# A graph layer's start-up: the last edge targets are converted in group 24, the first transfers change queues, and two filler matmuls go

## The chip, the cores and the metric

The kernel runs on one core of a Trainium2 chip. A core has a matrix engine (TensorE, PE in the profile; its weight loads are PEld), a vector engine (VectorE, DVE), a scalar engine (ScalarE, ACT), GpSimd (POOL) and a sync engine (SyncE, SP) that here only issues transfers. Each runs its own instructions in order, and they wait for one another on semaphores. DMAs are issued by SP, ACT and POOL and carried out by 16 DMA engines. The metric is the time of one execution on the device in microseconds (us); lower is better.

## The reference

Messages run along 25,000 edges between 50,000 nodes with 128 features, all float32. `dst` is sorted. What is computed, cut to its core:

```python
msg = jax.nn.relu(x[src] + edge_attr)                     # 25,000 x 128
agg = jax.ops.segment_sum(msg, dst, num_segments=50000)
h = x + agg
h = jax.nn.relu(jax.nn.relu(h @ W1 + b1) @ W2 + b2)       # 128 -> 256 -> 128
out = layernorm(x + h)                                    # eps 1e-5, no scale
```

## The kernel before

The nodes are cut into 131 groups: 130 of 384 nodes (three tiles of 128) and a last one of 80. The edges of a group lie in one stretch of the sorted list, and the kernel takes two windows of 128 edges for a group (one for the last group). Where the windows start depends on `dst`, so the kernel first has to search.

**The start-up.** `prepare` loads the first target of each of 125 rows of 200 edges (`dst_first`, line 396), the first target of each next row (`dst_next`, 232) and all the rows (`dst_rows`, 230). VectorE compares the first targets with the groups' first nodes (361 to 367) and marks the row in which each group begins (`row_holds`). TensorE picks these rows with two matmuls (421); ScalarE has converted the rows to floats for it (401). VectorE counts in them (289) and gets the window starts (382). GpSimd then fetches each window's (source, target) pairs (119). For groups 0 and 1 the windows are known beforehand: `first_pairs` holds the first 512 pairs, and GpSimd gathers their source rows at once (127). While it waits, TensorE runs fillers whose result nobody reads (`keep_busy`, 411): six matmuls of 128 columns on the identity before the search, three and one of 256 columns behind it.

**The main path**, for each group g. GpSimd gathers the source rows (113), SP loads `edge_attr` (107) and x (102). VectorE adds source rows and edge attributes (593), ScalarE takes the rectified sum rounded (`msg_hi`, 747), VectorE the rest (`msg_lo`, 600); in groups 0, 2 and 3 the second window isn't split but used whole (`msg_whole`, 607). TensorE transposes x into PSUM (838) and adds the messages by a product with 0/1 selection matrices (865; 861 for a whole part; 887 and 891 in group 1). ScalarE copies the sum to SBUF (`copy_hT`, 753), TensorE multiplies by W1 (the first layer, 901), ScalarE adds the bias and rectifies (759), TensorE multiplies by W2 (909), and VectorE adds the bias, x and takes the statistics (616, 628, 635, 644). ScalarE takes the root (764) and normalizes (778); SP stores (517). While group g's layers run, TensorE also transposes and sums group g + 1.

The order of work on each engine is written out by hand: as straight lines for the first groups, as a loop from group 2 or 3 on. On ScalarE the first groups read as follows, with the step that the change moves in the middle (lines 784 to 797):

```python
        high_part(1, 0)
        hidden(0, 0)
        source_nodes()
        hidden(0, 1)
        high_part(1, 1)
        act.wait_ge(c["last_pairs_loaded"], 16)
        nc.scalar.activation(c["last_dst"][:, :], c["last_pairs"][:, 1:2], ACT.Copy).then_inc(last_dst_ready, 1)
        copy_hT(1)
        hidden(1, 0)
```

`last_pairs` holds the pairs of the last 128 edges. SP loads it between the transfers of groups 3 and 4 (524). Its targets, converted to float (`last_dst`, 792), are needed on VectorE when it builds the last group's selection (573), and its sources by GpSimd for the last gather.

Of the kernel before, what the change touches and what calls it, by code (L numbers as in the profile page):

```python
# [8 lines left out]
ACT = mybir.ActivationFunctionType  # L9
# [12 lines left out]
EW = 128  # L22
# [9 lines left out]

ROWS = 125
TARGETS_FOUND, TARGETS_CHECKED, CHECKED = (12, 16), 20, 30
FAR = float(1 << 20)


# [5 lines left out]
FIRST_CHUNKS = 4  # L43
# [120 lines left out]
def prepare(nc, x, edge_attr, dst, pairs, w1, b1, w2, b2, c, sb, sem):  # L164

    edges, = dst.shape
    ROW = edges // ROWS
# [17 lines left out]
    dst_first = sb("dst_first", [ROWS, 1], INT32)  # L185
# [41 lines left out]
    flags_summed = sem("flags_summed")  # L227

    def prepare_sync(sp):
        sp.dma_start(dst_rows[:, :], dst.rearrange("(r e) -> r e", e=ROW)).then_inc(dst_loaded, 16)  # L230
        sp.wait_ge(next_cleared, 1)
        sp.dma_start(dst_next[0:ROWS - 1, :], bass.AP(dst.tensor, ROW, [[ROW, ROWS - 1], [1, 1]]),
                     allow_slow_non_contiguous=True).then_inc(next_loaded, 16)
        sp.dma_start(first_pairs[:, 1:FIRST_CHUNKS, :], pairs[EW:FIRST_CHUNKS * EW, :].rearrange("(k p) a -> p k a", p=EW),
                     allow_slow_non_contiguous=True).then_inc(more_pairs_loaded, 16)
        start_x(sp, x, 0, 0, c)
        start_edge_attr(sp, edge_attr, 0, 0, c)
        sp.dma_start(c["w1_sb"][:, :], w1).then_inc(w1_loaded, 16)
        for h in range(HC):
            sp.dma_start(c["b1_sb"][:, h:h + 1], b1[h * 128:(h + 1) * 128].rearrange("(p a) -> p a", a=1)).then_inc(w1_loaded, 16)  # L240

        sp.wait_ge(c["first_loaded"][0], 16)
        start_edge_attr(sp, edge_attr, 1, K * EW, c)
        start_x(sp, x, 1, 1, c)
        sp.dma_start(c["w2_sb"][:, :, :], w2.rearrange("(c p) n -> p c n", p=128)).then_inc(w2_loaded, 16)

        sp.wait_ge(c["window_loaded"], 16)
        sp.dma_start(b2_sb[:, 0, :], b2.rearrange("(a n) -> a n", a=1).to_broadcast([128, b2.shape[0]])).then_inc(c["b2_loaded"], 16)
# [144 lines left out]
    def prepare_scalar(act):  # L393

        act.dma_start(first_pairs[:, 0, :], pairs[0:EW, :]).then_inc(pairs_loaded, 16)
        act.dma_start(dst_first[:, :], bass.AP(dst.tensor, 0, [[ROW, ROWS], [1, 1]]),
                      allow_slow_non_contiguous=True).then_inc(first_loaded, 16)
        act.wait_ge(eps_ready, 1)
        nc.scalar.activation(table_mark[:, :], eps_col[:, :], ACT.Sqrt)
        act.wait_ge(dst_loaded, 16)  # L400
        nc.scalar.activation(dst_rows_f[:, 1:ROW + 1], dst_rows[:, :], ACT.Copy).then_inc(dst_f_ready, 1)
        act.wait_ge(pairs_loaded, 16)
        act.wait_ge(more_pairs_loaded, 16)
        nc.scalar.activation(first_dst[:, :], first_pairs[:, :, 1], ACT.Copy).then_inc(first_dst_ready, 1)

    def prepare_tensor(pe):
# [6 lines left out]
                                 start=True, stop=True)  # L413

        pe.wait_ge(ident_ready, 1)
        keep_busy(6, 128)
        pe.wait_ge(dst_f_ready, 1)
        pe.wait_ge(row_of_ready, 1)
        for k in range(K):
# [15 lines left out]
def main_path(nc, x, pairs, edge_attr, out, c, sb, sem, checks):  # L435
# [301 lines left out]
    def main_scalar(act):  # L737
# [50 lines left out]
        source_nodes()  # L788
        hidden(0, 1)
        high_part(1, 1)  # L790
        act.wait_ge(c["last_pairs_loaded"], 16)
        nc.scalar.activation(c["last_dst"][:, :], c["last_pairs"][:, 1:2], ACT.Copy).then_inc(last_dst_ready, 1)
        copy_hT(1)
        hidden(1, 0)
        high_part(2, 0)
# [8 lines left out]
        for g in range(3, LAST):  # L804
# [6 lines left out]
            for t in range(T):  # L811
                if inside(g - 3):
                    last = normalize(g - 3, t)
                if t == 0 and g == END:
                    deviation(LAST - 2)
                if t == 1 and inside(g + 2):
                    high_part(g + 2)
# [508 lines left out]
```

## Time and profile before

| | |
|---|---|
| three timed runs | 476.31, 475.66, 477.24 us (median 476.31) |
| the profiled execution | 476.41 us, its span 474.6 us |
| busy share of the span | PE 97%, PEld 80%, DVE 90%, ACT 91%, POOL 67% |
| chain that ended last | PE 94%, DVE 2%, issue 1%, ACT 1%, other 1% |
| granted TensorE clock, mean of the span | 0.989 |
| HBM traffic | 60.51 MB read, 25.60 MB written |

All rows come from the one profiled execution. A start is counted from the start of the span. A busy share close to 100% means that an engine works, not that it works at its peak. The chain is followed back from the last instruction, at each step to what released it; "issue" in it is time in which an engine waited for nothing that the profile shows. Matmuls of float32 operands appear as two records each.

### The profile page before, as it was taken

What the parts mean: (1) busy time and instruction counts of PE and PEld (TensorE: products, weight loads), DVE (VectorE), ACT (ScalarE), POOL (GpSimd) and SP (SyncE); (2) the same over time, 40 slices, a digit from 0 to 9 for tenths busy, and PEclk for the clock granted to TensorE, in tenths of its full rate; (3) what the DMA queues carried; (4) which work ended last, traced back from release to release, by engine and by line L of the source; (5) the groups of instructions that cost most, each with busy time, mean ns of one, the idle gap of its engine ahead of it and who ended that gap; (6) DMA issues with size and microseconds to landing.
All of it is one profiled execution on the core that took longest, in us unless ns stands there. A gap on an engine that the chain in (4) does not pass through costs nothing.

```text
span 474.6 us, 10056 instructions
## 1 busy us (share of the span) xinstructions
PE 458.8 (97%) x3037; PEld 380.3 (80%) x3037; DVE 426.8 (90%) x1761; ACT 431.0 (91%) x1047; POOL 317.0 (67%) x280
## 2 busy tenths in 40 slices
PE   7799999999999999998999999999999999999994
PEld 6678888888788888886888888888888888888883
DVE  6679999999999999996999999999999999999996
ACT  2359999999999999996999999999999999999995
POOL 6656766677677777655577777777777777777722
PEclk9899999999999999998999999999999999999998
DMA  5636666666666666665566666666666666666632
GB/s 125 190 89 189 201 182 202 194 197 190 197 183 197 189 199 187 195 194 155 170 191 186 199 203 186 197 191 200 185 200 189 199 189 191 195 194 196 190 118 88
DMA packets 83609, 86.77 MB, mean 183 GB/s; under 512 B 11767, under 2 KB 79252, under 8 KB 83556
## 3 DMA queue, kind: packets, MB, share of 16 engines
q1 hardware_dynamic: 74786, 68.76, 47.0%
q0 software_dynamic: 8496, 17.38, 13.4%
q8 instruction: 23, 0.38, 0.3%
q14 instruction: 30, 0.25, 0.2%
q10 hardware_dynamic: 274, 0.00, 0.0%
HBM read 60.51 MB, written 25.60 MB: 181 GB/s over the span
## 4 chain that ended last, share of the span: by engine, by line
PE 94%; DVE 2%; issue 1%; ACT 1%; another core or an unknown queue 1%; POOL 0%; POOLq 0%; DVEq 0%
PE h_ps L909 37%; PE h1T_ps L901 35%; PE hT_ps L865 12%; PE hT_ps L838 9%; PE h1T_ps L411 1%; PE spare_ps L861 0%; PE prep_ps L421 0%; DVE stats L635 0%; DVE h L616 0%; DVE z L628 0%; ACT hT L753 0%; ACT std L764 0%; DVE mean_var L644 0%; DVE msg_lo L600 0%
## 5 line engine op out<-in xcount | busy, mean ns | idle before, releaser
L113 POOL DMA_INDIRECT x_src<-in_x_dram,src_of x256 | 305.7, 1194 | 135.7 <-ACT hT L753 90.7
L909 PE MATMUL h_ps<-w_sb,h1T 128*128 128x128 f32 x1564 | 200.0, 278 | 0.4 <-ACT h1T L759 0.4
L901 PE MATMUL h1T_ps<-hT,w_sb 128*128 128x384 f32 (+1 forms) x524 | 190.4, 486 | 4.3 <-issue 2.9
L909 PEld LDWEIGHTS h_ps<-w_sb,h1T 128*128 128x128 f32 x1564 | 187.8, 194 | 0.7 <-ACT h1T L759 0.6
L778 ACT ACTIVATE y<-z,shift,rstd 128x128 f32<-128x128 f32 x384 | 172.3, 481 | 0.5 <-DVE shift L655 0.5
L759 ACT ACTIVATE h1T<-h1T_ps,b_sb 128x384 f32<-128x384 f32 (+1 forms) x262 | 151.1, 578 | 19.1 <-remote 2.3
L901 PEld LDWEIGHTS h1T_ps<-hT,w_sb 128*128 128x128 f32 x524 | 89.6, 191 | 39.4 <-issue 3.8
L616 DVE TENSOR_TENSOR h<-h_ps,b_sb 128x384 f32<-128x384 f32 x131 | 72.7, 555 | 35.1 <-PE h_ps L909 29.1
L635 DVE BATCH_NORM_STATS2 stats<-z 128x6 f32<-128x128 f32 x391 | 88.7, 282 | 0.1
L838 PEld LDWEIGHTS hT_ps<-ident,x_sb 128*128 128x128 f32 (+1 forms) x379 | 49.3, 140 | 39.6 <-issue 22.8
L576 DVE TENSOR_TENSOR sel<-node_in_range,dst_of 128x432 fp32r<-128x432 f32 x127 | 76.3, 601 | 0.0
L865 PE MATMUL hT_ps<-sel,msg_hi 128*128 128x216 f32 x250 | 71.4, 311 | 2.3 <-DVE msg_lo L600 2.3
L628 DVE SCALAR_TENSOR_TENSOR z<-h,x_sb 128x384 f32<-128x384 f32 x131 | 72.2, 551 | 0.0
L753 ACT ACTIVATE hT<-hT_ps 128x384 f32<-128x384 f32 x128 | 62.5, 488 | 2.3 <-issue 1.4
L865 PE MATMUL hT_ps<-sel,msg_lo 128*128 128x216 f32 x250 | 62.6, 276 | 0.0
L838 PE MATMUL hT_ps<-ident,x_sb 128*128 128x128 f32 (+1 forms) x379 | 62.1, 272 | 0.0
L747 ACT ACTIVATE msg_hi<-pre_msg 128x256 fp32r<-128x256 f32 (+1 forms) x132 | 54.3, 411 | 5.9 <-DVE pre_msg L593 5.7
L600 DVE SCALAR_TENSOR_TENSOR msg_lo<-pre_msg,msg_hi 128x256 fp32r<-128x256 f32 (+1 forms) x132 | 54.0, 409 | 4.7 <-ACT msg_hi L747 2.6
L593 DVE TENSOR_TENSOR pre_msg<-pre_msg,x_src 128x256 f32<-128x256 f32 (+1 forms) x135 | 51.8, 384 | 0.0
L865 PEld LDWEIGHTS hT_ps<-sel,msg_hi 128*128 128x128 f32 x250 | 47.8, 191 | 2.8 <-DVE msg_lo L600 2.8
L865 PEld LDWEIGHTS hT_ps<-sel,msg_lo 128*128 128x128 f32 x250 | 48.1, 193 | 0.0
L644 DVE BATCH_NORM_AGGREGATE mean_var<-stats 128x2 f32<-128x6 f32 x391 | 40.0, 157 | 0.2
(132 smaller groups left out, 142.3 us busy)
## 6 DMA issues: line engine op xcount, KB each, us to landing
x_sb<-in_x_dram SPq DMA_DIRECT2D x130, 192.0 KB
out_dram<-y SPq DMA_DIRECT2D x130, 192.0 KB
pre_msg<-in_edge_attr_dram SPq DMA_DIRECT2D x130, 128.0 KB
x_src<-in_x_dram,src_of POOLq DMA_INDIRECT x256
w_sb<-in_w_dram SPq DMA_DIRECT2D x2, 128.0 KB
dst_rows<-in_dst_dram SPq DMA_DIRECT2D x1, 97.7 KB
x_src<-in_x_dram,first_pairs POOLq DMA_INDIRECT x4, 2.8
b_sb<-in_b_dram SPq DMA_DIRECT2D x1, 64.0 KB
```

The costliest lines, as they stand in the source:

```text
L113: nc.gpsimd.indirect_dma_start(out=c["x_src"][:, g % EB, k, :], out_offset=None, in_=x, in_offset=bass.IndirectOffsetOnAxis(ap=index, axis ...
L576: nc.vector.tensor_tensor(sel[:, g % EB, :, :], node_in_range[:, :, :].to_broadcast([128, K, T * WP]), dst_of[:, g - FIRST_ROW:g - FIRST_R ...
L616: nc.vector.tensor_tensor(h2[0:p, g % 2, 0:n, :], h2_ps[g % 2][0:p, 0:n, :], b2_sb[0:p, :, :].to_broadcast([p, n, D]), ALU.add).then_inc(h ...
L628: nc.vector.scalar_tensor_tensor(z[0:p, g % ZB, 0:n, :], h2[0:p, g % 2, 0:n, :], 0.0, x_sb[0:p, g % XB, 0:n, :], ALU.max, ALU.add).then_in ...
L635: last = nc.vector.bn_stats(stats[0:p, g % SB, t, :], z[0:p, g % ZB, t, :])
L753: nc.scalar.activation(hT[:, 0:n, 0:p], sum_bank(g)[:, 0:n, 0:p], ACT.Copy).then_inc(hT_copied, 1)
L759: nc.scalar.activation(h1T[:, h, 0:n, 0:p], h1T_ps[h][:, 0:n, 0:p], ACT.Relu, bias=b1_sb[:, h:h + 1]).then_inc(h1_ready, 1)
L778: return nc.scalar.activation(y[0:p, g % YB, t, :], z[0:p, g % ZB, t, :], ACT.Identity, bias=shift[0:p, g % SB, t:t + 1], scale=rstd[0:p, ...
L838: nc.tensor.matmul(sum_bank(g)[:, t, 0:p], x_sb[0:p, g % XB, t, :], ident[0:p, 0:p], is_transpose=True, start=(t == 0), stop=False, skip_g ...
L865: last = nc.tensor.matmul(sum_bank(g)[:, 0:n, p0:p1], part[:, g % EB, k, :], cols, start=False, stop=final, skip_group_check=True)
L901: nc.tensor.matmul(h1T_ps[h][:, 0:n, 0:p], w1_sb[:, h * 128:(h + 1) * 128], hT[:, 0:n, 0:p], start=True, stop=True).then_inc(h1_summed, 1)
L909: last = nc.tensor.matmul(h2_ps[g % 2][0:p, t, :], h1T[:, h, t, 0:p], w2_sb[:, h, :], start=(h == 0 and t == 0), stop=(h == HC - 1), skip_ ...
```

## The change

Three edits, all in the order of work; no arithmetic is changed.

- The wait for `last_pairs` and the conversion to `last_dst` leave ScalarE's straight lines between `high_part(1, 1)` and `copy_hT(1)`. They now stand in ScalarE's loop, in the round of group 24, behind the first of group 21's three normalizations.
- `dst_first` goes from ScalarE's queue to the head of SP's, ahead of `dst_rows`. `dst_next` (with its wait for the cleared column) and the second load of `first_pairs` go from SP's queue to ScalarE's, behind the first load of `first_pairs` and ahead of ScalarE's first instruction.
- The fillers ahead of the search are four matmuls instead of six.

```diff
     def prepare_sync(sp):
+        sp.dma_start(dst_first[:, :], bass.AP(dst.tensor, 0, [[ROW, ROWS], [1, 1]]),
+                     allow_slow_non_contiguous=True).then_inc(first_loaded, 16)
         sp.dma_start(dst_rows[:, :], dst.rearrange("(r e) -> r e", e=ROW)).then_inc(dst_loaded, 16)
-        sp.wait_ge(next_cleared, 1)
-        sp.dma_start(dst_next[0:ROWS - 1, :], bass.AP(dst.tensor, ROW, [[ROW, ROWS - 1], [1, 1]]),
-                     allow_slow_non_contiguous=True).then_inc(next_loaded, 16)
-        sp.dma_start(first_pairs[:, 1:FIRST_CHUNKS, :], pairs[EW:FIRST_CHUNKS * EW, :].rearrange("(k p) a -> p k a", p=EW),
-                     allow_slow_non_contiguous=True).then_inc(more_pairs_loaded, 16)
         start_x(sp, x, 0, 0, c)
...
         act.dma_start(first_pairs[:, 0, :], pairs[0:EW, :]).then_inc(pairs_loaded, 16)
-        act.dma_start(dst_first[:, :], bass.AP(dst.tensor, 0, [[ROW, ROWS], [1, 1]]),
-                      allow_slow_non_contiguous=True).then_inc(first_loaded, 16)
+        act.wait_ge(next_cleared, 1)
+        act.dma_start(dst_next[0:ROWS - 1, :], bass.AP(dst.tensor, ROW, [[ROW, ROWS - 1], [1, 1]]),
+                      allow_slow_non_contiguous=True).then_inc(next_loaded, 16)
+        act.dma_start(first_pairs[:, 1:FIRST_CHUNKS, :], pairs[EW:FIRST_CHUNKS * EW, :].rearrange("(k p) a -> p k a", p=EW),
+                      allow_slow_non_contiguous=True).then_inc(more_pairs_loaded, 16)
...
         pe.wait_ge(ident_ready, 1)
-        keep_busy(6, 128)
+        keep_busy(4, 128)
...
-        act.wait_ge(c["last_pairs_loaded"], 16)
-        nc.scalar.activation(c["last_dst"][:, :], c["last_pairs"][:, 1:2], ACT.Copy).then_inc(last_dst_ready, 1)
         copy_hT(1)
...
             for t in range(T):
                 if inside(g - 3):
                     last = normalize(g - 3, t)
+                if t == 0 and g == LAST_DST_AT:
+                    act.wait_ge(c["last_pairs_loaded"], 16)
+                    nc.scalar.activation(c["last_dst"][:, :], c["last_pairs"][:, 1:2], ACT.Copy).then_inc(last_dst_ready, 1)
```

How the instructions stand on the engines. First ScalarE's program in the first groups, before: from group 1's second rounding to group 1's second hidden half (`hT<-prep_ps1` is the copy of group 1's sum).

```order
L747 ACTIVATE msg_hi<-pre_msg 128x128 [waits sum_ready]
L792 ACTIVATE last_dst<-last_pairs 128x1 [waits last_pairs_loaded]
L753 ACTIVATE hT<-prep_ps1 128x384 [waits hT_summed]
L759 ACTIVATE h1T<-h1T_ps0,b1_sb 128x384 [waits h1_summed]
L747 ACTIVATE msg_hi<-pre_msg 128x128 [waits sum_ready]
L759 ACTIVATE h1T<-h1T_ps1,b1_sb 128x384 [waits h1_summed]
```

The same place now:

```order
L748 ACTIVATE msg_hi<-pre_msg 128x128 [waits sum_ready]
L754 ACTIVATE hT<-prep_ps1 128x384 [waits hT_summed]
L760 ACTIVATE h1T<-h1T_ps0,b1_sb 128x384 [waits h1_summed]
L748 ACTIVATE msg_hi<-pre_msg 128x128 [waits sum_ready]
L760 ACTIVATE h1T<-h1T_ps1,b1_sb 128x384 [waits h1_summed]
```

The copy of group 1's sum now follows the rounding directly. Its new place on ScalarE, in the round of group 24, where `y` is the normalized output of group 21:

```order
L760 ACTIVATE h1T<-h1T_ps1,b1_sb 128x384 [waits h1_summed]
L765 ACTIVATE std<-mean_var,eps_col 128x3 [waits var_ready]
L754 ACTIVATE hT<-hT_ps 128x384 [waits hT_summed]
L779 ACTIVATE y<-z,shift,rstd 128x128 [waits shift_ready]
L815 ACTIVATE last_dst<-last_pairs 128x1 [waits last_pairs_loaded]
L779 ACTIVATE y<-z,shift,rstd 128x128
L748 ACTIVATE msg_hi<-pre_msg 128x256 [waits sum_ready]
```

One activation was put between the first and the second tile; nothing else moved there. Last the head of SP's program, before:

```order
L230 DMA dst_rows<-in_dst_dram 125x200
L232 DMA dst_next<-in_dst_dram 124x1 [waits next_cleared]
L234 DMA first_pairs<-in_pairs_dram 128x3x2
L102 DMA x_sb<-in_x_dram 128x384
L107 DMA pre_msg<-in_edge_attr_dram 128x2x128
```

and now, where the two transfers that left stand on ScalarE's queue behind `first_pairs<-in_pairs_dram 128x2`:

```order
L231 DMA dst_first<-in_dst_dram 125x1
L233 DMA dst_rows<-in_dst_dram 125x200
L103 DMA x_sb<-in_x_dram 128x384
L108 DMA pre_msg<-in_edge_attr_dram 128x2x128
L236 DMA w1_sb<-in_w1_dram 128x256
```

The rows have moved from the first place to the second, behind a load of 125 single elements; the loads of x and what follows have one transfer fewer ahead of them.

## Rows read from the trace of the kernel before

**Rows 1.** Stretch: us; busy PE, PEld, DVE, ACT, POOL; clock; DMA share; GB/s.

```profile
100.00:200.00 100.00, 100.00 (x679) 83.04 (x678) 93.27 (x383) 96.77 (x236) 71.43 (x59) 1.00 0.64 192
```

**Rows 2.** The chain that ended last: start, us, what.

```profile
16.43 2.90 issue
19.33 1.60 PE h1T_ps L901 x4
...
23.24 2.04 PE spare_ps L861 x2
...
25.85 1.56 PE h1T_ps L901 x4
...
28.62 0.43 PE prep_ps L861 x2
...
29.72 1.47 PE h1T_ps L901 x4
...
217.75 3.10 another core or an unknown queue
```

**Rows 3.** Timeline of TensorE, last addend of group 1's sum: start, us, what.

```profile
15.42 0.34 PE L891 MATMUL prep_ps<-second_sel,msg_lo 128*128 128x384 f32 x1
```

**Rows 4.** Timeline of ScalarE: the conversion, the copy of group 1's sum.

```profile
18.69 0.20 ACT L792 ACTIVATE last_dst<-last_pairs 128x1 f32<-128x1 int32 x1 [4.16 <-DMA last_pairs<-in_pairs_dram]
18.80 0.47 ACT L753 ACTIVATE hT<-prep_ps 128x384 f32<-128x384 f32 x1
```

**Rows 5.** Busy time by stretch, 22 to 24 us; columns as in rows 1.

```profile
22.00:24.00 2.00, 2.00 (x10) 1.95 (x9) 0.24 (x2) 0.00 (x0) 1.34 (x2) 0.50 0.54 152
```

**Rows 6.** Timeline of VectorE, group 2's messages and group 0's statistics.

```profile
18.21 0.28 DVE L593 TENSOR_TENSOR pre_msg<-pre_msg,x_src 128x128 f32<-128x128 f32 x1
18.41 0.67 DVE L635 BATCH_NORM_STATS2 stats<-z 128x6 f32<-128x128 f32 x3
21.09 0.29 DVE L600 SCALAR_TENSOR_TENSOR msg_lo<-pre_msg,msg_hi 128x128 fp32r<-128x128 f32 x1 [2.01 <-issue]
21.30 0.28 DVE L593 TENSOR_TENSOR pre_msg<-pre_msg,x_src 128x128 f32<-128x128 f32 x1
21.61 0.23 DVE L607 TENSOR_SCALAR msg_whole<-pre_msg 128x128 f32<-128x128 f32 x1
```

**Rows 7.** Timeline of GpSimd, the first gather of group 3.

```profile
16.38 0.94 POOL L113 DMA_INDIRECT x_src<-in_x_dram,src_of  x1 [0.30 <-issue]
```

**Rows 8.** Of the gathered rows' tile, 0 to 40 us: time to landing.

```profile
DMA to landing us min/median/max: 2.8/2.8/2.8
```

**Rows 9.** Timeline of all engines in the start-up; SPq and ACTq are issues.

```profile
0.75 0.40 SPq L230 DMA_DIRECT2D dst_rows<-in_dst_dram  x1
...
1.17 0.64 ACTq L396 DMA_DIRECT2D dst_first<-in_dst_dram  x1
...
2.16 2.93 PE L411 MATMUL h1T_ps<-ident 128*128 128x128 f32 x12 [2.16 <-POOL ident L260]
...
3.67 0.37 ACT L401 ACTIVATE dst_rows_f<-dst_rows 125x200 f32<-125x200 int32 x1 [0.34 <-DMA dst_rows<-in_dst_dram]
4.07 0.16 DVE L361 TENSOR_TENSOR first_of<-dst_first,lowest 125x1 f32<-125x1 int32 x1 [1.83 <-DMA dst_first<-in_dst_dram]
...
4.99 0.61 DVE L367 SCALAR_TENSOR_TENSOR row_holds<-node_row,next_of,row_before 125x128 f32<-125x128 f32 x2
...
5.49 1.68 PE L421 MATMUL prep_ps<-dst_rows_f,row_holds 125*128 125x201 f32 x4 [0.40 <-issue]
```

**Rows 10.** Timeline of TensorE, a full round's second layer, and first layers.

```profile
32.09 1.51 PE L909 MATMUL h_ps<-w_sb,h1T 128*128 128x128 f32 x12
...
214.31 1.46 PE L901 MATMUL h1T_ps<-hT,w_sb 128*128 128x384 f32 x4
...
217.71 1.46 PE L901 MATMUL h1T_ps<-hT,w_sb 128*128 128x384 f32 x4
...
225.16 1.64 PE L901 MATMUL h1T_ps<-hT,w_sb 128*128 128x384 f32 x4
```

More of the change, by code:

```diff
@@ L34 @@
 TARGETS_FOUND, TARGETS_CHECKED, CHECKED = (12, 16), 20, 30
+LAST_DST_AT = 24
 FAR = float(1 << 20)
```

## The prediction

> **What bounds the kernel now.** I read the long middle stretch first, then the chain of waits, then each engine's rows in the first 30 us. In the steady part TensorE is busy without a break at the full granted clock: 100.00 us of 100 [rows 1]. There a group costs what its matmuls cost, and nothing in this change touches them. So the change can act only where TensorE stands still: in the start-up and, perhaps, at one odd stop near 218 us. The chain shows both [rows 2]: 2.90 us of "issue" before the first layer of group 1 at 19.33, and 3.10 us at 217.75. After the start-up TensorE always has its next work, so what the start-up gains stays to the end.
>
> **The wait that goes.** The last addend of group 1's sum is issued at 15.42 and takes 0.34, so the sum is complete at 15.76 [rows 3]. Its copy out of PSUM starts on ScalarE only at 18.80, because ScalarE, in order, first stands 4.16 us for the last edge targets and converts them at 18.69 [rows 4]. TensorE has run out at 16.43 and starts group 1's first layer at 19.33 [rows 2], right behind the copy. With the conversion gone from there, the copy runs from about 15.8 to 16.3 (0.47) and TensorE goes on at about 16.45: 2.9 us are won on the spot.
>
> **What is late next.** With nothing late, TensorE needs from one first layer to the next 29.72 - 25.85 = 3.87 us here (group 2 to group 3) [rows 2]. Before, group 1 to group 2 took 25.85 - 19.33 = 6.52. In it, the clock stood at half (0.50 in 22 to 24 us) [rows 5], and the whole part of group 2's sum ended only at 25.28, a piece of 2.04 us where group 3's takes 0.43 [rows 2]. Both stand behind the long pause. Without the pause the next late thing is VectorE, whose work up to 19.1 doesn't hang on the copy: it adds the gathered rows of group 2 at 18.21 to 18.49, and its statistics end at 18.41 + 0.67 = 19.08 [rows 6]. ScalarE's rounding fits between. The low part then ends at about 19.08 + 0.29 = 19.37, the second half's addition (0.28) at 19.6 and the whole part (0.23) at 19.85 [rows 6]. In the unhindered spacing TensorE comes to the whole part 28.62 - 25.85 = 2.77 us after the first layer [rows 2], so at 19.22, and finds it 0.63 later. Group 2's first layer then starts at 16.45 + 3.87 + 0.6 = 20.9 instead of 25.85: **4.9 us earlier**. From group 2 to group 3 I keep 3.87.
>
> Could the gathers be too late? Group 3's first starts at 16.38 [rows 7], and a gather of the start lands 2.8 us after its start [rows 8]: landed at 19.2, wanted at about 20.2, after the whole part and group 0's aggregation. Group 3's second follows it on GpSimd and is wanted more than 2 us after it. Crowded DMA engines could eat the 1 us between; that goes into the range. Bounds of this part: 2.9 (only the pause goes, all the rest stays) and 5.5 (the 0.6 vanishes too).
>
> **The conversion in its new place.** It stands between two normalizations of group 24's round, where its input has been there for some 80 us, so it doesn't wait. It holds ScalarE for 18.80 - 18.69 = 0.11 us [rows 4]; ScalarE is idle 3.2 us of 100 [rows 1], which is 0.11 for each round of 3.40. Behind it stand a normalization and a rounding that nobody waits for at once. Cost 0, at most 0.1 once. The vector engine asks for its result in the last groups only.
>
> **The transfers of the start.** The first targets were issued by ScalarE's queue at 1.17 and VectorE used them at 4.07, 2.90 later; the rows of targets were issued at 0.75 and ScalarE took them at 3.67, 2.92 later [rows 9]. Now the first targets go at 0.75 and land at 3.65. The rows follow the 0.64 us of their issue, at 1.44, land at 4.36 and are converted (0.37) by 4.75. VectorE's path from the first targets to the first search matmul took 5.49 - 4.07 = 1.42; it now ends at 3.65 + 1.42 = 5.07, with the converted rows ready 0.3 before. **That is 0.42 earlier.** The next-row targets are issued at 1.17 on ScalarE's queue, about where SP had them, but no row shows when they landed, only that VectorE had them when it marked the rows at 4.99: at worst they hold the gain to nothing. Three more pairs follow at about 1.5, as before; the table load behind them starts some 0.1 later and hides before the rows land. The window fetch, the source nodes and the gathers all hang on this search and move along. I take 0.4, between 0 and 0.6.
>
> The Trainium skill says in "DMA: Bandwidth & Descriptors" (Issuing engines are not separate DMA queues) that DMAs issued from several engines end on the same 16 DMA engines, and that spreading them saves only issue time. By that rule the swap is worth the 0.42 of issue order and no more, and could be worth less if the rows crowd behind the first targets; this trace has no run with the other order.
>
> **The fillers.** Twelve records (two for each of six matmuls) take 2.93 us from 2.16, or 0.24 each, and the search starts at 5.49, 0.40 after them [rows 9]. Eight end at about 4.1. Nothing waits for them. With all twelve their end at 5.09 would just touch the new start at 5.07, so cutting two buys nothing by itself, and it leaves TensorE idle for 1.0 us instead of 0.4.
>
> **Sum.** 4.9 + 0.4 = 5.3. The profiled execution took 476.41 us with a span of 474.6; so a span of 469.3 and a time of 471.1. The median of the runs shown is 476.31, 0.1 below that execution: forecast **471.0 us**.
>
> **The rivals.**
> (a) *The fillers were needed.* The same shape of matmul in a full round takes 1.51 for twelve, half of the fillers' 2.93 [rows 9, 10]: TensorE's clock is at its lower level, 1.2 GHz, while the fillers run, and it rises to 2.4 GHz only after some work; the search still runs slowly (four passes in 1.68). With a pause of 1.0 us in that work the rise may come later, and the search, the transposes, the remaining fillers and the first sum go at half speed. Of the path from 7.2 to 10.7 at most all 3.5 us are doubled; much of it waits for VectorE anyway, so I take 2 (between 0 and 3.5): 473.0. Against it: about three quarters of the stretch stays full.
> The Trainium skill's "TensorE: Matmul & The Clock Gate" (Part 1) says that "the default state is throttled, and activity releases the throttle". By that, less early activity speaks for (a); if activity stays enough, it changes nothing, and by the one the time is 473.0, by the other 471.0.
> (b) *Something else stops group 2.* The piece of 2.04 us at 23.24 would be 0.86 at half clock (twice 0.43), so 1.2 us of it have another reason, which no row names [rows 2]; or a gather or its edge attributes land late among the crowded transfers. The 1.2 of the gain are given back: 472.2.
> (c) *The odd stop goes or doubles.* First layers stand at 217.71 and 225.16, 7.45 apart, where those at 214.31 and 217.71 are 3.40 apart: 4.05 us [rows 10]. The reason is unnamed. If it hangs on how instruction counts or transfers fall together, the change shifts that: 467.0 without it, 475.0 with a second one. For "it stays": the three timed runs lie within 1.6 us of each other.
> (d) *Slower.* The clock stays low not for one step but through the whole start-up. Every microsecond of TensorE work at the lower level costs another half of its duration; to lose more than the 5.3 gained, the rise, before done by about 7, must come after some 17. A delay of that size at 20 would give 477.8. Nothing in the trace shows such a long low stretch; the one after the pause lasted under 4 us.
> (e) *The change doesn't do what it says*, because copy or first layer wait for something hidden behind the conversion: 475.9. Against it: the sum is complete 3 us before.
>
> **Numbers.** Forecast 0.50; (a) 0.10; (b) 0.20; (c) 0.12 without the stop, 0.03 with two; (d) 0.03; (e) 0.02. The range runs from the case without the stop to (a) with more than its middle price: 467.0 to 473.8; the forecast's own range is 470.2 to 472.2. What a measurement can tell from no change is 0.3%, 1.4 us. All but (d), (e) and part of the doubled stop lie more than that below 476.3: faster 0.94, same 0.03, slower 0.03.
>
> **What would show it.** The copy of group 1's sum within 0.3 us of the sum's end, no 2.9 us before that first layer, a full granted clock from 14 to 30 us, group 3's first layer at about 24.4 instead of 29.72 (that is 5.3 earlier), the search at about 5.1, the rest of the trace shifted as a whole. The fillers are judged by the records of the search and of what follows: if those of 7 to 10 us still take their low-clock durations, (a) holds. Wrong would be a first layer of group 2 later than 22, or a shift that is lost again before 200 us.

## The result, and the profile after

The changed kernel is **slower**: 479.87 us median (476.59 to 480.74, 20 runs) against 476.38 (474.20 to 480.64, 20 runs) for the kernel before, a ratio of 1.0058 with the 95% interval 1.0038 to 1.0077. (A ratio here is estimated from the single runs and isn't the quotient of the two medians.) 471.0 was forecast, and the range ended at 473.8. The profiled execution took 480.18 us with a span of 478.2. (Lines of the changed kernel are one or two higher than those of before: L903 is the first layer, L754 the copy of a sum, L863 the whole part.)

The chain of waits of the kernel after (start, us, what):

```profile
1.19 3.43 DMA dst_next<-in_dst_dram
5.40 1.68 PE prep_ps L422 x4
7.72 2.56 PE h1T_ps L412 x6
13.34 1.53 PE h1T_ps L903 x4
18.37 1.67 PE h1T_ps L903 x4
22.09 5.14 another core or an unknown queue
27.79 2.93 PE h1T_ps L903 x4
33.53 1.47 PE h1T_ps L903 x4
...
221.26 3.05 another core or an unknown queue
```

Against [rows 2]: the 2.90 us of "issue" before group 1's first layer are gone, as forecast. In their place stand 5.14 us before group 2's, with a releaser that the profile can't name, and the first layer behind them takes 2.93 us where it took 1.56. The odd stop has stayed (3.05 at 221.26, 3.10 at 217.75 before). Group 3's first layer stands in the chain at 33.53 where it stood at 29.72 [rows 2], 3.8 us later, and about that much is carried to the end: the spans are 3.6 us apart, and in 100 to 200 us TensorE has 100.00 us of work, as before [rows 1].

The same stretch by ScalarE's and TensorE's timelines (start, duration, instruction, in brackets the idle time before it and its releaser):

```profile
17.74 0.49 ACT L754 ACTIVATE hT<-prep_ps 128x384 f32<-128x384 f32 x1 [1.27 <-issue]
27.25 0.49 ACT L754 ACTIVATE hT<-spare_ps 128x384 f32<-128x384 f32 x1 [5.16 <-remote]
```

```profile
17.37 0.34 PE L893 MATMUL prep_ps<-second_sel,msg_lo 128*128 128x384 f32 x1
...
18.29 1.56 PE L903 MATMUL h1T_ps<-hT,w_sb 128*128 128x384 f32 x4
...
21.96 0.63 PE L863 MATMUL spare_ps<-sel,msg_whole 128*128 128x216 f32 x2
22.43 0.83 PE L911 MATMUL h_ps<-w_sb,h1T 128*128 128x128 f32 x6
27.79 2.93 PE L903 MATMUL h1T_ps<-hT,w_sb 128*128 128x384 f32 x4 [4.53 <-ACT hT L754]
```

The copy of group 1's sum starts 0.03 us after the sum is done (17.71; before: 15.76 and 18.80 [rows 3, 4]). But group 2's sum, recorded as done at 22.59, is copied at 27.25 only, 4.66 us later. GpSimd's last gather before that starts at 24.66 and takes 0.94 us. The kernel before had the same on a smaller scale, which neither [rows 2] nor [rows 5] shows. From its timelines, GpSimd's last gather in that stretch, the whole part that completes group 2's sum, and the copy of this sum:

```profile
22.70 0.94 POOL L113 DMA_INDIRECT x_src<-in_x_dram,src_of  x1 [0.30 <-issue]
23.04 0.95 PE L861 MATMUL spare_ps<-sel,msg_whole 128*128 128x216 f32 x2
25.31 0.49 ACT L753 ACTIVATE hT<-spare_ps 128x384 f32<-128x384 f32 x1 [3.76 <-PE spare_ps L861]
```

There the sum was recorded as done at 23.99, 1.3 us ahead of its copy. Back to the changed kernel: what the engines do meanwhile, by stretches (columns as in [rows 1]):

```profile
22.00:24.00 2.00, 1.26 (x8) 1.07 (x8) 0.10 (x1) 0.09 (x1) 1.53 (x2) 1.00 0.73 223
24.00:26.00 2.00, 0.00 (x0) 0.00 (x0) 0.00 (x0) 0.00 (x0) 1.30 (x2) 0.73 0.16 39
26.00:28.00 2.00, 0.21 (x1) 0.21 (x2) 0.56 (x1) 0.49 (x1) 0.00 (x0) 0.50 0.13 33
28.00:30.00 2.00, 2.00 (x4) 1.09 (x5) 0.00 (x0) 0.52 (x2) 1.69 (x2) 0.50 0.16 39
30.00:32.00 2.00, 2.00 (x11) 1.59 (x9) 1.64 (x7) 1.02 (x4) 0.21 (x1) 0.56 0.13 35
```

From 24 to 26 us nobody works but GpSimd, which starts gathers (1.30 us). The granted clock goes to 0.50, the 1.2 GHz level, at about 24.9, when TensorE has had no work since 23.26, and stays there until about 31.7. Of these 6.8 us TensorE works from 27.79 on, 4.0 us. Before, the low stretch was 20.7 to 24.1 ([rows 5] shows its middle), 3.4 us with TensorE at work throughout, and it lay ahead of a copy that came 1.3 us after its sum in any case.

The start-up, all engines (the last line is of the kernel before, the same fillers behind the search):

```profile
2.17 2.08 PE L412 MATMUL h1T_ps<-ident 128*128 128x128 f32 x8 [2.17 <-POOL ident L258]
2.66 0.16 DVE L359 TENSOR_TENSOR first_of<-dst_first,lowest 125x1 f32<-125x1 int32 x1 [0.42 <-DMA dst_first<-in_dst_dram]
4.44 0.37 ACT L402 ACTIVATE dst_rows_f<-dst_rows 125x200 f32<-125x200 int32 x1 [0.63 <-DMA dst_rows<-in_dst_dram]
4.71 0.16 DVE L362 TENSOR_TENSOR next_of<-dst_next,highest 125x1 f32<-125x1 int32 x1 [1.50 <-DMA dst_next<-in_dst_dram]
5.40 1.68 PE L422 MATMUL prep_ps<-dst_rows_f,row_holds 125*128 125x201 f32 x4 [1.16 <-DVE row_holds L365]
7.51 2.77 PE L412 MATMUL h1T_ps<-x_sb,ident 128*128 128x256 f32 x6
...
7.34 1.46 PE L411 MATMUL h1T_ps<-x_sb,ident 128*128 128x256 f32 x6
```

The first targets are used at 2.66 (4.07 before [rows 9]), but now the next-row targets come last, at 4.71, and the search starts at 5.40 instead of 5.49 [rows 9]: 0.09 us won, 0.42 forecast. The six records of fillers behind the search take 2.77 us at the low level; in the execution of before they took 1.46. Group 0's first layer is at 13.34 instead of 11.40.

### The profile page after: what moved, and what is told of

The parts are those of the page before. It is cut to its first block, busy times and chain, and to the rows that moved or that the text cites. A ratio compares the mean times of both kernels' runs of the same rounds, so it can differ in the third digit from the quotient of the medians.

```text
span 478.2 us, 10048 instructions
## 1 busy us (share of the span) xinstructions
PE 460.4 (96%) x3033; PEld 379.7 (79%) x3033; DVE 426.5 (89%) x1761; ACT 431.5 (90%) x1047; POOL 317.5 (66%) x280
## 4 chain that ended last, share of the span: by engine, by line
PE 94%; DVE 2%; another core or an unknown queue 2%; ACT 1%; DMA 1%; issue 0%; ACTq 0%; DVEq 0%
PE h_ps L911 36%; PE h1T_ps L903 35%; PE hT_ps L867 11%; PE hT_ps L840 8%; PE h1T_ps L412 1%; DMA dst_next<-in_dst_dram 1%; ACT h1T L760 0%; PE prep_ps L422 0%; DVE stats L636 0%; DVE h L617 0%; DVE z L629 0%; ACT hT L754 0%; ACT std L765 0%; DVE mean_var L645 0%
## 5 line engine op out<-in xcount | busy, mean ns | idle before, releaser
L903 PE MATMUL h1T_ps<-hT,w_sb 128*128 128x384 f32 (+1 forms) x524 | 192.5, 490 | 4.9 <-ACT hT L754 4.9
L903 PEld LDWEIGHTS h1T_ps<-hT,w_sb 128*128 128x128 f32 x524 | 90.4, 193 | 40.6 <-ACT hT L754 4.7
L754 ACT ACTIVATE hT<-hT_ps 128x384 f32<-128x384 f32 x128 | 62.6, 489 | 2.3 <-PE hT_ps L881 1.6
```

The costliest lines, as they stand in the source:

```text
L754: nc.scalar.activation(hT[:, 0:n, 0:p], sum_bank(g)[:, 0:n, 0:p], ACT.Copy).then_inc(hT_copied, 1)
L903: nc.tensor.matmul(h1T_ps[h][:, 0:n, 0:p], w1_sb[:, h * 128:(h + 1) * 128], hT[:, 0:n, 0:p], start=True, stop=True).then_inc(h1_summed, 1)
```

## The experiments

Every kernel here was timed in 12 runs (r4: 7) on a chip that ran the kernel before 30 to 35 times between them. The median of before was 476.47 for the e series, 477.27 for p, 476.72 for q and 476.39 for r. A ratio is to the kernel before of the same series; differences of medians between series are not used.

**First series: which part costs.** e1 has the conversion's edit alone:

```diff
         high_part(1, 1)
-        act.wait_ge(c["last_pairs_loaded"], 16)
-        nc.scalar.activation(c["last_dst"][:, :], c["last_pairs"][:, 1:2], ACT.Copy).then_inc(last_dst_ready, 1)
         copy_hT(1)
...
                     last = normalize(g - 3, t)
+                if t == 0 and g == LAST_DST_AT:
+                    act.wait_ge(c["last_pairs_loaded"], 16)
+                    nc.scalar.activation(c["last_dst"][:, :], c["last_pairs"][:, 1:2], ACT.Copy).then_inc(last_dst_ready, 1)
```

> Only the conversion moves. Theory 'late results': TensorE's results are held back until about 1.6 us after GpSimd's run of eight gathers without a pause (before: gathers from 13.87 to 23.64, results at 25.28; after: 15.80 to 25.60, results at 27.23). The gathers don't move here, so group 2's first layer stays at 25.7 to 26.0 although group 1's starts 2.8 us earlier, at 16.5; ratio 0.998 to 1.004. Rival 'the wait was the cost' (as forecast): group 2's first layer at 21 and 4.9 us less, ratio 0.990.

Measured: 479.00, ratio 1.0038 (1.0003 to 1.0074). The conversion's removal alone makes the kernel slower, though the interval only just leaves out no change. e2 changes the fillers alone:

```diff
-        keep_busy(6, 128)
+        keep_busy(4, 128)
```

> Only two fillers fewer. Theory 'clock': the rise comes one step later in most executions (10.7 instead of 7.0), window start product at 10.2 instead of 8.7, everything behind it 1.9 us later, ratio 1.003 to 1.008. Rival: fillers are free, ratio 1.000, and the late rise of the changed kernel came from another edit.

Measured: 479.06, ratio 1.0056 (1.0019 to 1.0093). First layers of groups 0 to 3 stood at 12.62, 19.31, 27.18 and 33.84. e3 changes the queues alone:

```diff
-        keep_busy(4, 128)
+        keep_busy(6, 128)
...
         high_part(1, 1)
+        act.wait_ge(c["last_pairs_loaded"], 16)
+        nc.scalar.activation(c["last_dst"][:, :], c["last_pairs"][:, 1:2], ACT.Copy).then_inc(last_dst_ready, 1)
```

(against the changed kernel; the conversion's later place is taken out again).

> Only the transfers change queues. The next-row targets land at 4.65 as in the changed kernel (issue 0.63 instead of 0.28), so the search starts at 5.3 to 5.4, 0.1 earlier than before: ratio 0.999 to 1.001. Rival 'the swap is itself a loss': the later pairs delay gather 1 from 4.97 to 5.67 and that reaches the end, ratio 1.002 or more.

Measured: 476.74, ratio 0.998 (0.9942 to 1.0018): no difference. e4 is the changed kernel with six fillers:

```diff
-        keep_busy(4, 128)
+        keep_busy(6, 128)
```

> The changed kernel with six fillers again. Theory 'clock' plus 'late results': the clock rises at 7, the start is as before, group 1's first layer at 16.4, results held back until 25.2: ratio 0.998 to 1.004. Rival (only the fillers were wrong): 5.3 us less than before, ratio 0.989.

Measured: 479.07, ratio 1.0038 (1.0003 to 1.0074), with group 0's first layer at 10.91 and yet group 2's at 25.47. So the late group 2 isn't a matter of the start. (e4 can't be told from the changed kernel by its time, 1.0038 against 1.0058: what four fillers add on top of the moved conversion isn't shown.) The chain of e1 shows where its gain goes:

```profile
16.43 1.72 PE h1T_ps L903 x4
...
18.95 2.03 another core or an unknown queue
...
21.58 3.81 another core or an unknown queue
25.39 0.02 issue
25.41 0.50 ACT hT L754
...
25.95 2.92 PE h1T_ps L903 x4
```

Group 1's first layer is 3.0 us earlier (16.34), group 2's is not earlier at all (25.95, before 25.85), and group 3's is later (32.07). In all these kernels the copy of group 2's sum came 1.6 to 1.8 us after the same thing had ended: GpSimd's run of eight gathers, back to back, for groups 2 to 5. News is late inside the run too: the 2.03 us at 18.95 are ScalarE's wait for the second hidden half of group 1, whose matmuls had ended at 17.90 and which started at 21.00. And only TensorE's news is late. In the same stretch of e1 VectorE's `msg_lo` (19.03) followed ScalarE's `msg_hi` (done at 18.95) by 0.08 us, and TensorE's whole part (20.02) followed VectorE's operand (done at 19.96) by 0.06. That is the theory of the next series: *while GpSimd starts gathers without a break, ScalarE and VectorE hear late that TensorE is done*.

**Second series: shorten the run, lengthen it, fill the wait.** p1 (on e1) and p2 (on before) let group 5's gathers wait for the copy of group 2:

```diff
-            back = g - GATHER_AHEAD
+            back = g - (3 if g == 5 else GATHER_AHEAD)
```

> The kernel before with only the conversion moved, and GpSimd's two gathers of group 5 wait for the copy of group 2 instead of group 1. Theory (TensorE's results of group 2 are held until GpSimd's run of back-to-back gathers is over, and come some 1.65 us after it): the run is six gathers long and ends at about 21.2 us instead of 23.65, so hT of group 2 is copied at about 22.9 (with the conversion alone: 25.41), its first layer starts near 23.4 instead of 25.95, and the time comes down by 2 us or more, to about 474 to 476.5. Rival (the wait has nothing to do with the gathers): copy at 25.4 as before, 479.

> The kernel before with GpSimd's gathers of group 5 behind the copy of group 2, nothing else. Theory (results held by the run of gathers): hT of group 2, which was copied at 25.31 us, 1.66 us after the run ended, is copied as soon as its sum is done, near 24.4; the time falls by up to 1 us, to about 475.5. Rival (no hold): copy at 25.3, 476.4.

Measured: p1 476.17, ratio 0.996 (0.9924 to 0.9995); p2 475.56, ratio 0.9947 (0.9919 to 0.9975). p1's last gather of the run and its copy of group 2:

```profile
19.72 0.95 POOL L114 DMA_INDIRECT x_src<-in_x_dram,src_of  x1 [0.30 <-issue]
22.86 0.95 POOL L114 DMA_INDIRECT x_src<-in_x_dram,src_of  x1 [2.20 <-ACT hT L754]
```

```profile
22.10 0.49 ACT L754 ACTIVATE hT<-spare_ps 128x384 f32<-128x384 f32 x1 [1.00 <-PE spare_ps L863]
```

The second row is group 5's first gather, which now waits. The copy comes 3.3 us before e1's 25.41 (0.5 of it because this execution's gathers began that much earlier). For p2 I expected the copy near 24.4; it was at 23.83, 3.1 us after the run, with its own sum as the releaser, and the ratio fell by more than the 1 us expected. Both got a second stop later: the copy of group 4 waited for a run of the gathers of groups 5 to 7.

p3 puts one more gather into the run of e1:

```diff
+        nc.gpsimd.indirect_dma_start(
+            out=x_spare[:, :], out_offset=None, in_=x,
+            in_offset=bass.IndirectOffsetOnAxis(ap=c["src_of"][:, 0, 0:1], axis=0)).then_inc(spare_loaded, 16)
         for g in range(4, GROUPS):
```

> The kernel before with only the conversion moved, and one more gather (128 rows of x into a tile that nobody reads) between those of group 3 and group 4. Theory (results held by the run of gathers): the run has nine gathers and ends at about 24.9, so hT of group 2 is copied at about 26.65 instead of 25.41 and its first layer starts near 27.2; the time is 1.2 us above that of the conversion alone, about 480.2. Rival (the wait has nothing to do with the gathers): copy at 25.4, 479.

```profile
26.38 0.49 ACT L759 ACTIVATE hT<-spare_ps 128x384 f32<-128x384 f32 x1 [5.24 <-remote]
```

Measured from the first gather of the run (13.41; e1: 13.86), the copy came after 12.97 us instead of 11.55: 1.42 us later for a gather of 1.25 us. The time was 479.57, ratio 1.004 (1.0011 to 1.0069): slower than before, but not the 1.2 us above e1's ratio that I expected; that part missed.

p4 keeps TensorE at work in the wait of e1:

```diff
             output_sum(g, 1)
+            if g == 1:
+                for _ in range(12):
+                    nc.tensor.matmul(hT_ps[:, 0:2, :].rearrange("p t n -> p (t n)"), ident[:, :], w1_sb[:, 0:256], start=True, stop=True)
```

> The kernel before with only the conversion moved, and twelve filler matmuls of 128x256 on TensorE between group 1's second layer and group 2's first, about 3.1 us at full clock, into a bank that nobody uses then. Theory (the held results make TensorE idle for 3.4 us, and the low clock that follows, 6.8 us over dense work, costs what the conversion won): the first layer of group 2 still starts near 26, but takes 1.56 us instead of 2.92, group 3's starts near 29.8 instead of 32.07, and the time is about 476.4 to 477 instead of 479. Rival (the low clock is not what costs): group 3's first layer at 32 and 479. If the results were not held but only recorded late, group 2's first layer would start behind the fillers, near 25.7, too.

```profile
22.25 0.63 PE L863 MATMUL spare_ps<-sel,msg_whole 128*128 128x216 f32 x2
23.90 0.94 PE L911 MATMUL h_ps<-w_sb,h1T 128*128 128x128 f32 x6 [1.02 <-issue]
24.67 5.35 PE L942 MATMUL hT_ps<-w_sb,ident 128*128 128x256 f32 x24
29.86 1.45 PE L903 MATMUL h1T_ps<-hT,w_sb 128*128 128x384 f32 x4
```

```profile
27.63 0.49 ACT L754 ACTIVATE hT<-spare_ps 128x384 f32<-128x384 f32 x1 [3.78 <-remote]
```

Two things stand here. From 23.90 on TensorE works through the wait without a break, while the copy of a sum that it ended at 22.88 starts at 27.63: TensorE isn't stopped, the news of its work is late. And the first layer behind takes 1.45 us instead of 2.92. From the copy of group 2 to group 3's first layer it took 33.53 - 27.63 = 5.90 us, of which 1.74 are fillers beyond the end of the copy (28.12 to 29.86); without them 4.16, where e1 took 32.07 - 25.41 = 6.66. **The low clock cost e1 2.5 us here.** The "6.8 us over dense work" of the expectation is the whole low stretch of e1, 24.1 to 30.9; TensorE worked in it from 25.95 on, 4.9 us, and half of that is the same 2.5. I had counted the fillers at one pass each; they are two, and took 5.35 us instead of 3.1. The time was 477.78, ratio 1.0009 (0.9974 to 1.0044), so the timed runs alone don't tell it from e1.

**Third series: is it the gathers, and what is the change worth without the stop?** q1 (on e1), q2 (on before) and q3 (on the changed kernel) pace all groups:

```diff
-GATHER_AHEAD = 4
+GATHER_AHEAD = 3
```

> The kernel before with only the conversion moved, and GATHER_AHEAD = 3 instead of 4 for every group (gathers of group g wait for the copy of group g-3), so that no run of gathers is longer than six and none follows at groups 5 to 7. Theory (results are held by long runs of gathers): group 2's copy as in the paced kernel, 22.1 us, and the second hold (hT of group 4 copied at 31.57 there, 0.76 late) is gone as well; time 475 to 476, at or a little under the 476.2 of the paced kernel. Rival (with two gathers for each group 3.4 us later, data come late somewhere): over 477.

> The kernel before with GATHER_AHEAD = 3, nothing else. With group 5's gathers paced it was 0.9947 of before, and one hold of 2.12 us came later (at 31.08, behind the six gathers of groups 5 to 7). Theory: that hold is gone, the time is 474 to 475.5. Rival: no change from pacing further, 475.6 or more.

> The changed kernel whole (conversion moved, queues exchanged, four fillers) with GATHER_AHEAD = 3. If the change lost only because of the held results, it is now at or under the kernel before with the same GATHER_AHEAD (475 or less). If the four fillers cost by themselves (the rise of the clock near 10.7 us instead of 7, +1.9 us), it is about 1 to 2 us above the conversion alone with GATHER_AHEAD = 3, about 477.

Measured: q1 474.32, ratio 0.993 (0.9893 to 0.9967); q2 474.75, 0.9943 (0.9915 to 0.9972); q3 475.39, 0.9953 (0.9921 to 0.9984). All three beat the kernel before, and among them no difference can be told. (q1 came out below the 475 to 476 expected, q2 as expected, q3 between its two cases.) q4 adds six iotas to p1, so that GpSimd stays busy behind its run of six:

```diff
                 start_gather(nc, x, g, k, xsrc_loaded[g % EB], c)
+            if g == 4:
+                for i in range(6):
+                    nc.gpsimd.iota(counted[:, i, :], pattern=[[1, 384]], base=0, channel_multiplier=0,
+                                   allow_small_or_imprecise_dtypes=True)
```

> The kernel with the conversion moved and group 5's gathers behind the copy of group 2, and on GpSimd six iotas of 128x384 (0.46 us each, 2.5 us in all, written to a tile nobody reads) right behind group 4's gathers: GpSimd is busy as long as with eight gathers, but the run of gathers has six. If the gathers hold TensorE's results, hT of group 2 is copied at about 22.1 to 22.5 us as without the iotas, and the time is about 476.2; if GpSimd's being busy does, it is copied near 24.5, and the time is about 478.5.

```profile
19.82 0.95 POOL L114 DMA_INDIRECT x_src<-in_x_dram,src_of  x1 [0.30 <-issue]
20.77 2.48 POOL L556 IOTA counted<- 128x384 f32 x6
```

```profile
22.17 0.49 ACT L759 ACTIVATE hT<-spare_ps 128x384 f32<-128x384 f32 x1 [1.01 <-remote]
```

The copy comes 1.40 us after the last gather, in the middle of the iotas: the gathers hold the news, not a busy GpSimd. The time, 478.69 (ratio 1.0018, 0.9982 to 1.0053), is above my 476.2: the iotas pushed the gathers behind them into a new run of eight (23.41 to 33.75), and the chain shows 3.34 us of unknown wait at 31.48.

**Fourth series: a run of four.** Runs of six still ended 1.4 us before the copy. r1 (on e1), r2 (on before) and r4 (on e4) let group 4's gathers wait for the copy of group 2 and later ones for three groups back; r3 is r1 with group 5 two back as well:

```diff
-            back = g - GATHER_AHEAD
+            back = g - (2 if g == 4 else 3)
...
+            back = g - (2 if g in (4, 5) else 3)
```

> The kernel before with the conversion moved; the gathers of group 4 wait for the copy of group 2, those of every later group g for the copy of group g-3, so that the run of gathers at the start has four instead of eight. So far group 2's copy came 1.28 to 1.43 us after a run of six and 1.65 us after one of eight. Theory (held by the run, whatever its length): with four the run ends at 18.3, and the copy comes when the sum itself is done, near 20 to 20.6 (with a run of six: 22.1), group 2's first layer near 21, and the time is 2 us under that of the same pacing without the conversion moved, about 472.5. Rival (runs of six and less hold nothing, the conversion is worth little for another reason): no better than with runs of six, 474 to 475.5, and within 1 us of its partner without the conversion moved.

> The same pacing (group 4's gathers behind the copy of group 2, later ones three groups behind) on the kernel before, conversion where it was: group 1's first layer stays near 18.9 and group 2's near 24.4. Theory: 474.7, as with GATHER_AHEAD = 3, and 2 us above its partner with the conversion moved. Rival: the two within 1 us of each other.

> As the first of these (conversion moved, four gathers in the first run), but group 5's gathers wait for the copy of group 3, so that the second run has two gathers instead of four. If the second run of four also holds results (copy of group 3 late), this is better by up to 1 us; if the later gathers come late for group 5's messages, it is worse by about 1.5 us (a stall before the copy of group 5, near 33 us).

> The changed kernel with six fillers instead of four (conversion moved, queues exchanged) and the four-gather pacing. Theory: as the first of these, about 472.5, since the exchange of queues was neutral (0.998) in its own run. If the later gathers of groups 0 and 1 that the exchange brought cost something once nothing else holds, it is 0.5 to 0.7 us above.

Measured: r1 473.95, ratio 0.9962 (0.9935 to 0.9988); r2 475.28, 0.9989 (0.9965 to 1.0013); r3 474.27, 0.9973 (0.995 to 0.9995); r4 472.81, 0.9939 (0.9915 to 0.9963). r1's first layers on TensorE, then r2's:

```profile
15.88 1.56 PE L903 MATMUL h1T_ps<-hT,w_sb 128*128 128x384 f32 x4
...
20.51 1.56 PE L903 MATMUL h1T_ps<-hT,w_sb 128*128 128x384 f32 x4
...
24.29 1.56 PE L903 MATMUL h1T_ps<-hT,w_sb 128*128 128x384 f32 x4
29.88 1.56 PE L903 MATMUL h1T_ps<-hT,w_sb 128*128 128x384 f32 x4 [1.62 <-ACT hT L754]
```

```profile
19.64 1.56 PE L901 MATMUL h1T_ps<-hT,w_sb 128*128 128x384 f32 x4 [2.74 <-issue]
23.43 1.56 PE L901 MATMUL h1T_ps<-hT,w_sb 128*128 128x384 f32 x4
27.22 1.56 PE L901 MATMUL h1T_ps<-hT,w_sb 128*128 128x384 f32 x4
32.69 1.56 PE L901 MATMUL h1T_ps<-hT,w_sb 128*128 128x384 f32 x4 [1.50 <-ACT hT L753]
```

Here the conversion's gain is seen: group 3's first layer stands at 24.29 with the conversion moved and 27.22 without. 0.93 of that is r2's later start (group 0's first layer at 11.87, r1's at 10.94), so 2.0 are the conversion's. Group 2's first layer of r2 stood at 23.43, where 24.4 was expected. The medians are 1.33 us apart, between the 2 us of the one theory and the "within 1" of the other, and the two ratios' intervals overlap: the trace shows the gain, the timed runs don't settle its size. The gathers of groups 4 to 6 make a second run of six, and the copy of group 4 came 1.12 us after its end; r3, meant to break that, got a run of six one group later (its copy 1.17 us after the end), and its time can't be told from r1's. A run of four isn't free of it either: in r4 ScalarE's second hidden half of group 1 waited 0.67 us for TensorE's news and started at 19.52, 0.96 us after the run's end. r4, the changed kernel with six fillers and paced gathers, has the lowest median of its series (in seven runs); q1's ratio can't be told from it.

**The copy of group 2's sum against the run of gathers**, all by the profiled executions, from the start of the run's first gather:

```text
run of 9   p3                             12.97 us
run of 8   before, after, e1, e2, e3,     11.44, 11.45, 11.55, 11.56, 11.54,
           e4, p4                         11.56, 11.58
run of 6   p1, q1, q2, q3, q4              8.75,  8.66,  8.62,  8.65,  8.71
run of 4   r1, r3, r4                      6.56,  7.26,  6.57 (their sums end then)
```

Left out are p2 and r2, where the late conversion made the sum itself the last thing. The first gather's start differs by up to 2.7 us between these executions, and for group 1's first layer there are kernels with the conversion early and late in each row but the first and the last: the copy moves with the gathers, not with TensorE's work. Runs of four tell nothing here, since the sum was last.

**The same steps in every trace, and the odd stop.** The timelines of the 18 profiled executions (the kernel before, the changed one, and the experiments) call 71 waits of ScalarE and VectorE "remote". Each of them ends 1.42 to 1.46 us times a whole number after the first gather of its run: 4.3 and 5.7 (steps 3 and 4), 7.1 to 7.3 (5), 8.5 to 8.7 (6), 11.4 to 11.7 (8), 13.0 (9), and none comes later than the step that is the number of gathers in the run. A gather follows the one before after 1.25 us, so the news falls further behind with every gather. Half of these waits (36) are the odd stop. From the timelines of GpSimd and ScalarE before, the first and the last gather of a run of five, and the wait:

```profile
213.75 0.94 POOL L113 DMA_INDIRECT x_src<-in_x_dram,src_of  x1 [2.06 <-issue]
218.86 0.94 POOL L113 DMA_INDIRECT x_src<-in_x_dram,src_of  x1 [0.30 <-issue]
220.91 1.05 ACT L759 ACTIVATE h1T<-h1T_ps,b_sb 128x384 f32<-128x384 f32 x2 [2.33 <-remote]
```

In all 18 executions GpSimd first stands about 2.05 us for a reason that the profile doesn't show, then catches up with five gathers back to back, and ScalarE and VectorE go on 1.0 to 1.2 us after the last. The same happens with GATHER_AHEAD = 3. So the 4.05 us of [rows 10] look like the same late news; no run here takes the five gathers apart, so this is read from the timing and not shown by an experiment.

## Why the prediction was wrong

**The wait that goes**: right. The copy of group 1's sum follows the sum, and 3.0 us are won before group 1's first layer (16.34 instead of 19.33 in e1; in the changed kernel 18.29 for a start that came 1.9 later).

**What is late next**: here it failed. The step said that the whole part waits 0.63 us for VectorE and that group 2's first layer then starts at 20.9, 4.9 us earlier. VectorE did come about as forecast (its whole operand in e1 at 19.96, forecast 19.85), and the sum was recorded as done at 20.65 there and at 22.59 in the changed kernel. But the next late thing was the news of it, which came 1.6 to 1.8 us after the end of GpSimd's run of eight gathers. That had been so before, too: the copy at 25.31 was 1.67 us behind the run's end, and only the late conversion had covered it. So of the 4.9 us nothing reached group 2. The clue was in the trace: the piece of 2.04 us ends at 25.28 in the chain, but the matmuls in it were over at 23.99 by the timeline, so the whole part did not end "only at 25.28", as the prediction has it. Rival (b) named this piece and priced it at 1.2, as a part of the work, where it was the visible end of a second limit that stood under the whole stretch. I asked of the gathers whether their data land in time, and not what starting them does to the others.

**The clock**: the prediction took the low clock of [rows 5] as a consequence of the pause that would go with it. The pause didn't go; it moved behind group 1's work, joined the wait for the news, and became one idle time of 4.53 us. The low level then lay over dense work with nothing left to hide it: 4.0 us in the changed kernel, 4.9 in e1. p4 puts this at 2.5 us in e1, and group 3's first layer was 2.4 later there than before (32.07, 29.64 by the timeline). That makes the conversion's removal slower than nothing, and not merely worth nothing.

**Rival (a), the fillers**: it came true. In the profiled execution it is +1.9 us (priced at 2), and in the timed runs four fillers alone cost 0.56% (e2), 2.7 us. How sure the late rise of the clock is with four, few executions tell. Of the 15 profiled executions with six fillers, group 0's first layer stood between 10.85 and 13.59, at 11.57 in the mean; in the three with four, at 12.06, 12.62 and 13.34, 12.67 in the mean. With six, the six records behind the search took 1.46 to 1.62 us in twelve executions, and 2.38, 2.54 and 2.77 in q1, q2 and p4; with four, 1.94, 2.37 and 2.77. So all three executions with four have the slow records, and three of fifteen with six. The start-up of e2's profiled execution was only 1.2 us late; the rest fits what the conversion did: the gathers and so group 2 moved back, group 1 did not (19.31), the idle time between them grew.

**The transfers of the start**: 0.09 instead of 0.42. The first targets came sooner than forecast (used at 2.66, forecast 3.65), and their issue took 0.40 us on SP, not the 0.64 it had on ScalarE. But the next-row targets, of which I wrote that no row shows when they landed, set the end: their issue took 0.63 us on ScalarE's queue (0.28 on SP before), behind another of 0.39, and they were used at 4.71. The lower bound, nothing, was the right value. e3 agrees (0.998).

The Trainium skill says in "DMA: Bandwidth & Descriptors" (Issuing engines are not separate DMA queues) that spreading issues over engines saves issue time only. The trace agrees for the search, which moved by 0.09 us, less than any issue time here. For the first targets alone it doesn't: they were issued 0.41 us earlier and used 1.41 us earlier.

**The odd stop**: stayed, as forecast. Its reason was "unnamed"; by the timing it is the same late news behind a run of five gathers, so the limit that sank the forecast stood twice in the trace of before. **Where the conversion stands now**: 0.19 us at 108.12 and no wait, as forecast.

**The range** gave every second limit a price of at most 2 us of the gain, and slower a chance of 0.03. It held no case in which a removed wait only uncovers another that had been there all along, with the idle time now in a worse place. One sum in rival (d) is off by a little: a rise that comes 13 us later costs 6.5 us, and 471.0 + 6.5 is 477.5, not 477.8.

What stays open: by what path gathers delay the news of TensorE's work, why it moves in steps of 1.43 us, and why GpSimd stands for 2.05 us before the odd stop. Shown are the dose (runs of six, eight and nine), that iotas of the same length don't do it, and that TensorE itself runs on.

## What to carry to other kernels

When a wait is removed, look for a second one under it: an unexplained piece in the chain just behind the wait is a sign of it, and it must be priced as a limit for the whole stretch, not as a part of the work. Idle time that only moves can cost more where it lands, since the low clock that follows it may fall on dense work. In a start-up full of indirect gathers, start those that are needed and let the later ones wait for a consumer's progress: one constant, GATHER_AHEAD = 3 instead of 4, was worth 0.6% (q2), as much as the whole change lost. It shortens the runs at the start only, not the run of five at the odd stop.

## What the runs showed of the hardware

- Long runs of back-to-back gathers on GpSimd (1.25 us each) delay what ScalarE and VectorE hear of TensorE's work. Nine held a sum's copy until 1.94 us after their end, eight until 1.57 to 1.76 after, six until 1.00 to 1.43, five (at the odd stop) until 1.01 to 1.23; counted from the first gather, 1.42 to 1.46 us for each. News between ScalarE and VectorE and from VectorE to TensorE came within 0.1 us in the same stretch (e1). Pairs in the steady part held nothing that could be seen. The profile calls such waits "another core", "an unknown queue" or "remote".
- The rise of TensorE's clock at the start is uncertain from execution to execution: with the same six fillers the six records behind the search took 1.46 to 1.62 us in twelve executions and 2.38 to 2.77 in three.
- The price of an issue differs with its queue: the strided load of 124 next-row targets took 0.63 us on ScalarE's queue and 0.28 on SP's before, the second there in both; that of the 125 first targets 0.64 on ScalarE's [rows 9] as the second, and 0.40 on SP's as the first.
